# Attention's outputs packed by DMA and scaled by GpSimd, masks of bank-filling diagonals moved to VectorE, joined programs, and expert 0's places and lists first

## The chip, the cores and the metric

The kernel runs on one core of one Trainium2 chip, as one launch. The metric is the device time of that core in microseconds. Times of before come from three runs; the profile is of one further execution.

## The reference

Four residual blocks follow one another on x of shape [4, 1024, 256], each on a layer norm of x. The first is a mamba scan (512 inner channels, 16 states), the second a top-2 mixture of eight experts, the third causal attention with grouped heads, the fourth a mixture in which each expert takes its 256 best tokens per batch. Only the last two are touched:

```python
# attention: 16 query heads, 4 key heads, 16 channels each
q = rope((x @ Wqa @ Wqb).reshape(b, s, 16, 16)); k, v = ...   # k with rope
scores = where(causal, -inf, q @ k^T * 16 ** -0.5)
x = x + (softmax(scores) @ v).reshape(b, s, 256) @ Wout + bout
# experts: each of 8 takes its 256 highest tokens per batch
probs = softmax(layernorm(x) @ gate_w)
top_p, top_idx = top_k(probs transposed to [b, e, t], 256)
y = gelu(xn[top_idx] @ w1) @ w2 * top_p
x = x + zeros.at[top_idx].add(y)
```

## The kernel before

The kernel is written with one program per engine and semaphores between them; a stage is a block, and all engines meet at its end. Around some stages stands a `cleanup_on_exit`, which frees and resets what the stage held. The order of the work within a stage is written out by hand.

The stages are: mamba (to 1015 us of the span), the top-2 experts (to 1336), `norm_project` (norm, q, k, v and rope, written to DRAM in parts, to 1452), `attention` (1456 to 1953), `project_scores` (output projection, the next norm, gate scores, 1954 to 2013), and `choose_experts` (the search for each expert's threshold, places and lists, then the loop over eight experts, to the end).

**Attention** runs 16 units, one for each batch and key head (`w = 4 b + kv`), each with four query heads. A unit has 12 steps x: for the first half of the queries (h = 0) four key tiles, for the second half (h = 1) eight. At a step PE makes transposed scores for two pairs of heads (`scores_t`, L2293), ACT takes the exponential into `pt` (L2346), GpSimd cuts the future out of diagonal tiles (L2230), and PE weighs v with it into bank OB (`weigh_v`, L2309). Column 16 of v is one, so the sums come with the outputs, as the 17th of each head's 32 rows. At x = 4, and at x = 0 of the next unit, ACT copies the bank to `ot` [128, 1024] (`copy_out`, L2336), half at a time.

Between these, in three slots of each step, PE makes "pieces" for the next unit: untransposed scores of 512 columns or fewer in three banks (`maxima_scores`, L2249). A piece that touches a diagonal gets the mask added by a second matmul (L2252). DVE reduces each piece to a maximum (`take_max`, L2364) and frees its bank. `unit_events` lays the pieces and turns in order, and SHARES says how many events each step gets. Among the events are the two o_turns of a unit: PE transposes four 128x128 tiles of `ot` (`turn_out`, L2268), and DVE takes the reciprocal of the sums and multiplies (`divide_out`, L2394 and L2396) into `o_all` by rows of tokens. The maxima are cut into bf16 parts, sent to DRAM and back as extra rows of Q by SP (`send_maxima`, L2204 and L2206), and SP loads the heads of later units (`load_heads`).

**project_scores** turns each of the 32 tiles of `o_all` on PE (`turn_o`, L2479), ACT copies it (`copy_oT`, L2546), PE multiplies by w_out (`project`, L2487), and DVE adds to X and takes the statistics (L2593, L2597). PE may be two tiles ahead of the adds.

**choose_experts** searches the thresholds over 15 digits: DVE compares all tokens with three trial levels (L2948), in two halves of four tiles, PE counts by matmuls with ones (L2774), DVE picks the digit (L2951 to L2964). Then for all eight experts at once DVE finds members (L2971), PE ranks them (L2779, L2780), DVE makes places from these (L2979 to L3000) and, with GpSimd for the second half of the tokens, values (L3006, L3008; L3098, L3100). One-hots and lists for expert 0 follow (L3014, L2856), GpSimd gathers its rows (L3113), and PE begins the loop at L2799. That loop is bound by PE to the end.

Of the kernel before, what the change touches and what calls it, by code (L numbers as in the profile page):

```python
# [629 lines left out]
NE = 8  # L630
# [1089 lines left out]
def norm_project(nc, g, load_from, v_all, heads, q_dram, k_dram, weights, ahead):  # L1720
    with ExitStack() as ctx:
# [28 lines left out]
        t_psum, part_act, part_dve, out_sem = n.sem("t_psum"), n.sem("part_act"), n.sem("part_dve"), [n.sem(f"out_parts{i}") for i in range(2)]  # L1750
# [10 lines left out]
        def _(sp):  # L1761
# [34 lines left out]
            for s in range(2):  # L1796
                sp.wait_ge(out_sem[s], 8 * NB3 * NCH)

# [300 lines left out]
SHARES = (3, 3, 5, 2, 3, 5, 4, 4, 5, 3, 3, 2)  # L2099
SLOTS = 3  # L2100

# [5 lines left out]
def unit_events(w):  # L2107

    if w + 1 == NU:
        return [[[("m_turn", w, 1)], [], []], [[], [], [("o_turn", w - 1, 1)]]] + [[[], [], []] for _ in range(3)] + \  # L2110
            [[[], [], [("o_turn", w, 0)]]] + [[[], [], []] for _ in range(NSTEP - 6)]
    events = maxima_of(w + 1, 0) + maxima_of(w + 1, 1)
    events.insert(16, ("o_turn", w, 0))
    events.insert(18, ("m_turn", w + 1, 0))
    events.insert(1, ("m_turn", w, 1))
    events.insert(6, ("o_turn", w - 1, 1) if w else None)
    out, at = [], 0
    for share in SHARES:
        mine = events[at:at + share]
        out.append([[e for e in mine[share * i // SLOTS:share * (i + 1) // SLOTS] if e] for i in range(SLOTS)])  # L2120
        at += share
    assert at == len(events)
    return out

def schedule():

    units = [unit_events(w) for w in range(NU)]
    fill = maxima_of(0, 0) + [("m_turn", 0, 0)] + maxima_of(0, 1)
    ending = [("o_turn", NU - 1, 1)]  # L2130
    in_order = fill + [e for unit in units for step in unit for slot in step for e in slot] + ending
    return fill, units, ending, {e: k for k, e in enumerate(in_order)}

def attention_weights(n, g):
    mask_f = n.sb("mask_f", [P, P])
# [19 lines left out]
def attention(nc, g, v_all, heads, o_all, w_out, q_dram, k_dram, m_dram, weights):  # L2156
    with ExitStack() as ctx:
# [8 lines left out]
        ot = n.sb("ot", [P, SEQ])  # L2166
# [4 lines left out]
        inv = n.sb("inv", [P, KB, GH])  # L2171

# [10 lines left out]
        fill, in_unit, ending, order = schedule()  # L2183
# [15 lines left out]
        def _(sp):  # L2199
# [9 lines left out]
            send_maxima(0, 0)  # L2209
            sp.dma_start(w_out[:, :, :], g["wout"].rearrange("(k p) c -> p k c", p=P)).then_inc(w_loaded, 16)  # L2210
            for w in range(NU):
                send_maxima(w, 1)
                if w + NKV - 1 < NU:
# [3 lines left out]
                if w + 1 < NU:  # L2217
                    send_maxima(w + 1, 0)
            sp.wait_ge(w_loaded, 16)

        @block.gpsimd
        def _(pool):
            loads.wait(pool)
            for w in range(NU):
                for x in range(NSTEP):
                    if on_diagonal(x):
                        for pair in range(2):
# [3 lines left out]
                                               channel_multiplier=-1).then_inc(future_cut, 1)  # L2231
                for t in (2 * w, 2 * w + 1):
                    pool.tensor_tensor(X[:, t, :], X[:, t, :], bout[:, :], ALU.add).then_inc(x_biased, 1)

        @block.tensor
        def _(pe):
# [3 lines left out]
            def maxima_scores(w, h, i, k):  # L2240
# [5 lines left out]
                k0, diagonal = part * BANK, (tile + 1) * P - part * BANK <= BANK  # L2246
# [17 lines left out]
            def turn_out(w, h, k):  # L2264
                pe.wait_ge(ot_copied, 2 * w + h + 1)
                for i in range(4):
                    at = h * BANK + i * P
                    mm = pe.transpose(PS[:, k % NSB, i * P:(i + 1) * P], ot[:, at:at + P], ident[:, :])  # L2268
                mm.then_inc(piece_made, 1)

            def pieces(events):
                for e in events:
# [5 lines left out]
                    elif e[0] == "m_turn":  # L2278
                        turn_maxima(*e[1:], k)
                    else:  # L2280
                        turn_out(*e[1:], k)
# [16 lines left out]
            def weigh_v(w, x):  # L2298

                (b, kv), (h, kb) = divmod(w, NKV), STEPS[x]  # L2300
                if kb == 0 and (w or h):
                    pe.wait_ge(ot_copied, 2 * w + h)
# [24 lines left out]
            pieces(ending)  # L2327

        @block.scalar
        def _(act):  # L2330
            def copy_out(w, h):

                act.wait_ge(pv_done, NSTEP * w + (HK if h == 0 else NSTEP))
                if w:
                    act.wait_ge(o_step, 2 * w + h - 1)
                act.activation(ot[:, h * BANK:(h + 1) * BANK], PS[:, OB, :], ACT.Copy).then_inc(ot_copied, 1)  # L2336
# [18 lines left out]
        def _(dve):  # L2355
            dve.tensor_copy(ident_b[:, :], ident[:, :]).then_inc(consts, 1)
            loads.wait(dve)
            dve.tensor_copy(mask[:, :], mask_f[:, :]).then_inc(consts, 1)  # L2358
# [29 lines left out]
            def divide_out(w, h, k):  # L2388

                b, kv = divmod(w, NKV)  # L2390
                src = PS[:, k % NSB, :].rearrange("p (i j c) -> p i j c", i=4, j=GH)
                to = slice(h * 4, h * 4 + 4)
                tiles = slice(b * KB + h * 4, b * KB + h * 4 + 4)
                dve.reciprocal(inv[:, to, :], src[:, :, :, HD]).then_inc(o_step, 1)  # L2394
                dve.wait_ge(o_step, 2 * w + h + 1)
                dve.tensor_tensor(o_all[:, tiles, kv * GH * HD:(kv + 1) * GH * HD].rearrange("p i (j d) -> p i j d", j=GH),  # L2396
                                  src[:, :, :, 0:HD], inv[:, to, :, None].to_broadcast([P, 4, GH, HD]),
                                  ALU.mult).then_inc(piece_read, 1)

            def pieces(events):  # L2400
                for e in events:
# [6 lines left out]
                    elif e[0] == "m_turn":  # L2408
                        cut(*e[1:], k)
                    else:  # L2410
                        divide_out(*e[1:], k)
# [6 lines left out]
            pieces(ending)  # L2418

def project_scores(nc, g, o_all, w_out, xnT, xn_all, rows_to, gate, ahead):
    with ExitStack() as ctx:
# [3 lines left out]
        oT = n.sb("oT", [P, 2, KC, P])  # L2426
# [3 lines left out]
        oT_psum, oT_copied, o_psum, o_added = (n.sem(x) for x in ("oT_psum", "oT_copied", "o_psum", "o_added"))  # L2430
# [6 lines left out]
        TURN_BANKS, GB, OTB, OB = 3, 3, 4, 6  # L2437
# [36 lines left out]
        def _(pe):  # L2474
            def turn_o(t):
                if t >= 2:
                    pe.wait_ge(oT_copied, t - 1)
                for c in range(KC):
                    mm = pe.transpose(PS[:, OTB + t % 2, c * P:(c + 1) * P], o_all[:, t, c * P:(c + 1) * P], ident[:, :])  # L2479
                mm.then_inc(oT_psum, 1)  # L2480

            def project(t):
                pe.wait_ge(oT_copied, t + 1)
                if t >= 2:
                    pe.wait_ge(o_added, t - 1)
                for c in range(KC):
                    mm = pe.matmul(PS[:, OB + t % 2, 0:DM], oT[:, t % 2, c, :], w_out[:, c, :], start=c == 0, stop=c == KC - 1)  # L2487
# [36 lines left out]
            turn_o(0)  # L2524
            for t in range(NT):
                if t + 1 < NT:
                    turn_o(t + 1)
# [13 lines left out]
        def _(act):  # L2541
            def copy_oT(t):
                act.wait_ge(oT_psum, t + 1)
                if t >= 2:
                    act.wait_ge(o_psum, t - 1)
                act.activation(oT[:, t % 2, :, :].rearrange("p c x -> p (c x)"), PS[:, OTB + t % 2, 0:KC * P],  # L2546
# [768 lines left out]
```

## Time and profile before

| | us |
|---|---|
| median of 3 runs | 2563.05 |
| lowest, highest | 2562.51, 2564.99 |
| the profiled execution | 2565.26 |
| its span | 2563.5 |
| mean granted clock of PE over the span | 0.946 |

The profile is of a single execution. Instructions are named by engine, line and operation, with what they write and read. PE is the matmul engine, DVE VectorE, ACT ScalarE, POOL GpSimd, SP the engine that issues most DMAs. The start of an instruction is measured from the start of the span. PE's ends are modelled, so starts are surer than ends.

### The profile page before, as it was taken

The page shows a single profiled execution, that of the slowest core. Times are in us where ns is not written, and L with a number is a line of the kernel's source. Part 1 is how long each engine was busy: PE and PEld are TensorE (multiplying, and loading weights), DVE is VectorE, ACT ScalarE, POOL GpSimd, SP SyncE. Part 2 cuts the span into 40 slices and gives each one's busy share as a digit, 9 for nine tenths or more (in the row PEclk, how much of TensorE's full clock was granted, in tenths as well). Part 3 has the DMA queues.
Part 4 walks back from the last instruction along what each step waited for, and adds up shares of the span by engine and source line. Part 5 has one row for each costly group of instructions (what it writes and reads, how often), then busy time and mean ns, then how long its engine had stood idle before and what let it go on. Part 6 is the DMA issues. An engine that isn't in the chain of part 4 may idle for free. (4 is left out here: it accounts for less than half of the span.)

```text
span 2563.5 us, 35108 instructions
## 1 busy us (share of the span) xinstructions
PE 2265.3 (88%) x11484; PEld 1336.4 (52%) x11485; DVE 1779.8 (69%) x2586; ACT 1340.3 (52%) x2581; POOL 1346.8 (53%) x1026
## 2 busy tenths in 40 slices
PE   8995889989989987699977699999998559999998
PEld 3442444544544544699964344444445326666666
DVE  6998999999999997655557788888883741111100
ACT  4777887788788785322225456666665211111110
POOL 1545999899899894377756222222222123333432
PEclk9997999999999999799987799999999769999999
DMA  5357345125124113644446522222200503333322
GB/s 164 146 188 259 105 133 186 46 79 172 50 92 155 50 50 103 175 73 70 72 87 142 130 34 33 36 44 36 34 3 4 198 25 67 82 70 68 74 51 25
DMA packets 149681, 231.17 MB, mean 90 GB/s; under 512 B 26257, under 2 KB 98897, under 8 KB 149394
## 3 DMA queue, kind: packets, MB, share of 16 engines
q1 hardware_dynamic: 120258, 190.25, 24.7%
q0 software_dynamic: 29280, 39.11, 9.5%
q8 instruction: 79, 1.29, 0.2%
q14 instruction: 64, 0.52, 0.1%
HBM read 152.23 MB, written 81.66 MB: 91 GB/s over the span
## 5 line engine op out<-in xcount | busy, mean ns | idle before, releaser
L1263 POOL TENSOR_TENSOR scan_hC<-scan_h,scan_c_all 128x1024 f32<-128x1024 f32 x256 | 613.0, 2420 | 65.1 <-DVE scan_h L1118 63.8
L1118 DVE TENSOR_TENSOR_SCAN scan_h<-scan_dA,banks 128x1024 f32<-128x1024 f32 x224 | 504.6, 2276 | 21.6 <-ACT scan_dA L1040 12.9
L893 PE MATMUL banks<-scan_hC,all_ident 128*128 128x512 f32 x1024 | 487.5, 600 | 26.4 <-DVE scan_xc L1125 26.4
L2346 ACT ACTIVATE attn_pt<-banks 128x1024 f32<-128x1024 f32 (+3 forms) x384 | 292.3, 810 | 186.3 <-PE banks L2293 184.8
L1033 ACT ACTIVATE scan_scaled<-mamba_duT,mamba_bT 128x128 f32<-128x128 f32 x1024 | 312.0, 388 | 22.7 <-PE banks L870 22.3
L2230 POOL TENSOR_SCALAR_AFFINE_SELECT attn_pt<-attn_pt 128x256 f32<-128x256 f32 x256 | 104.2, 413 | 382.4 <-ACT attn_pt L2346 380.8
L2364 DVE TENSOR_REDUCE attn_m_lo<-banks 128x1 f32<-128x512 f32 (+3 forms) x432 | 266.8, 662 | 30.1 <-PE banks L2249 19.9
L893 PEld LDWEIGHTS banks<-scan_hC,all_ident 128*128 128x128 f32 x1024 | 185.3, 191 | 179.3 <-issue 129.2
L3068 DVE TENSOR_TENSOR ffn_y<-banks,ffn_gates 128x512 f32<-128x512 f32 x32 | 22.1, 692 | 334.2 <-PE banks L2828 327.5
L3124 POOL DMA_INDIRECT out<-ffn_y,ffn_ids x64 | 105.3, 1646 | 270.4 <-DVE ffn_y L3068 260.6
L2249 PE MATMUL banks<-attn_K,attn_Q 96*128 96x512 bf16 (+3 forms) x768 | 232.1, 340 | 11.1 <-DVE attn_mask L2358 10.0
L2812 PE MATMUL banks<-ffn_xgT,ffn_w 128*128 128x512 f32 x512 | 229.0, 599 | 0.8 <-issue 0.8
L2828 PE MATMUL banks<-ffn_w,ffn_hT 128*128 128x256 f32 x1024 | 228.6, 380 | 0.0
L2828 PEld LDWEIGHTS banks<-ffn_w,ffn_hT 128*128 128x128 f32 x1024 | 191.9, 190 | 28.5 <-issue 4.3
L2293 PE MATMUL banks<-attn_Q,attn_K 99*128 99x512 bf16 (+3 forms) x768 | 182.9, 327 | 1.2 <-ACT attn_pt L2346 1.1
L2886 ACT ACTIVATE ffn_hT<-banks 128x1024 f32<-128x1024 f32 x64 | 65.5, 1024 | 210.4 <-PE banks L2812 200.8
L870 PEld LDWEIGHTS banks<-all_ident,scan_scaled 128*128 128x128 f32 x1024 | 118.8, 144 | 104.2 <-DVE scan_h L1118 73.4
L2309 PE MATMUL banks<-attn_pt,attn_v_all 128*32 128x512 f32 (+3 forms) x1536 | 163.6, 498 | 0.7 <-POOL attn_pt L2230 0.6
L2249 PEld LDWEIGHTS banks<-attn_K,attn_Q 96*128 96x128 bf16 x768 | 74.2, 98 | 168.3 <-DVE attn_m_lo L2364 71.2
L870 PE MATMUL banks<-all_ident,scan_scaled 128*128 128x128 f32 x1024 | 141.5, 283 | 18.2 <-DVE scan_h L1118 16.7
L1040 ACT ACTIVATE scan_dA<-mamba_dt,mamba_a_neg 128x1024 f32<-128x1024 f32 x112 | 127.2, 1144 | 53.7 <-DVE scan_h L1118 46.0
L2812 PEld LDWEIGHTS banks<-ffn_xgT,ffn_w 128*128 128x128 f32 x512 | 96.1, 191 | 107.4 <-issue 106.7
(353 smaller groups left out, 3851.2 us busy)
## 6 DMA issues: line engine op xcount, KB each, us to landing
scan_c_all<-scratch_bc SPq DMA_DIRECT2D x64, 512.0 KB, 6.2
ffn_w<-in_e_w SPq DMA_DIRECT2D x16, 1024.0 KB, 5.4
attn_Q<-scratch_q SPq DMA_DIRECT2D x96, 128.0 KB, 4.1
scratch_x<-front_xc SPq DMA_DIRECT2D x8, 1024.0 KB, 5.8
scratch_z<-front_zs SPq DMA_DIRECT2D x8, 1024.0 KB, 7.5
scan_xc<-scratch_x SPq DMA_DIRECT2D x16, 512.0 KB, 3.7
scan_zs<-scratch_z SPq DMA_DIRECT2D x16, 512.0 KB, 4.7
scratch_dt<-front_lw SPq DMA_DIRECT2D x7, 1024.0 KB, 4.1
```

The costliest lines, as they stand in the source:

```text
L870: mm = pe.transpose(PS[:, (s % 2) * HALVES + half, i * P:(i + 1) * P], scaled[:, half * TPB // HALVES + i, :], ident[:, :])
L893: mm = pe.matmul(PS[:, YB + i, :], ident[:, :], hC[:, u % NHC, i * BANK:(i + 1) * BANK], start=s == 0, stop=s == NST - 1, skip_group_check ...
L1033: op = act.activation(scaled[:, t, :], duT[:, t, :], ACT.Copy, scale=bT[:, t, i:i + 1])
L1118: dve.tensor_tensor_scan(h[:, u % NH, :], decay, drive, 0.0, ALU.mult, ALU.add).then_inc(scanned, 1)
L1263: pool.tensor_tensor(hC[:, u % NHC, :], h[:, u % NH, :], c_all[:, s, :], ALU.mult).then_inc(hC_done, 1)
L2249: mm = pe.matmul(PS[:, k % NSB, at:at + width], Q[0:KR, kv, j0 + z, tile * P:(tile + 1) * P], K[0:KR, kv, k0:k0 + width], start=True, stop ...
L2293: mm = pe.matmul(PS[:, ST + 2 * pair + z, 0:BANK - lo], K[:, kv, kb * P:(kb + 1) * P], Q[:, kv, 2 * pair + z, h * BANK + lo:(h + 1) * BANK ...
L2309: mm = pe.matmul(PS[j * VW:(j + 1) * VW, OB, lo:BANK], v_all[:, b * KB + kb, kv, :], pt[:, (NSTEP * w + x) % 4, j, 0:BANK - lo], start=kb ...
L2346: act.activation(pt[:, at % 4, 2 * pair:2 * pair + 2, 0:width], PS[:, ST + 2 * pair:ST + 2 * pair + 2, 0:width], ACT.Exp, scale=HD ** -0.5 ...
L2364: dve.tensor_reduce(dst, PS[:, k % NSB, 0:nj * width].rearrange("p (j x) -> p j x", j=nj), AX, ALU.max).then_inc(piece_read, 1)
L2812: mm = pe.matmul(PS[:, HB + (hp % 2) * 2 + i, :], w1[:, s, k, (2 * hp + i) * P:(2 * hp + i + 1) * P], xgT[:, pr, k, :], start=k == 0, stop ...
L2828: mm = pe.matmul(PS[:, YB + z, hf * DM:(hf + 1) * DM], hT[:, pr, c, j * P:(j + 1) * P], w2[:, s, c, :], start=c == 0, stop=c == HC - 1, sk ...
```

## The change

1. **Outputs of attention.** `turn_out` and `divide_out` are gone from attention, `turn_o` and `copy_oT` from project_scores. A class `HeadOutputs` takes their place. SP sends `ot` of a unit to DRAM (`send`, 512 KB) and takes it back by eight DMAs (`take`): the 16 rows of each head into `dense`, which has channels on partitions, and the row of sums, repeated over 16 partitions, into `sums`. DVE inverts `sums` in place, 64 partitions × 1024 elements (`invert`), for unit w − 2 after step x = 4 of unit w; the last two after tiles 8 and 12 of project_scores. GpSimd multiplies (`scale`), at the same place in its own order, and the last two at the head of project_scores. ACT's `copy_out` waits for the last unit's store. `project` reads `dense` as it is and waits, every eight tiles, until four units are scaled.
2. **Masks.** For pieces whose diagonal ends with the bank (tiles 3 and 7, eight pieces a unit) PE adds no mask; DVE does both in one tensor_tensor_reduce with a mask of 512 columns, of which the first 384 are zero.
3. **Wait moved.** SP's wait for norm_project's stores stands now in attention, ahead of the load of w_out.
4. **Choice.** The trial is compared in 6 + 2 tiles. `places(q)` runs for expert 0 alone, then for the other seven; between them stand expert 0's lists. All values are made on DVE.
5. **Programs.** top2, attention and lists stand in one cleanup instead of three.

```diff
@@ def unit_events(w):
     events = maxima_of(w + 1, 0) + maxima_of(w + 1, 1)
-    events.insert(16, ("o_turn", w, 0))
-    events.insert(18, ("m_turn", w + 1, 0))
+    events.insert(17, ("m_turn", w + 1, 0))
     events.insert(1, ("m_turn", w, 1))
-    events.insert(6, ("o_turn", w - 1, 1) if w else None)
-SHARES = (3, 3, 5, 2, 3, 5, 4, 4, 5, 3, 3, 2)
+SHARES = (3, 3, 4, 2, 3, 4, 4, 4, 5, 3, 3, 2)
+class HeadOutputs:
+    def send(self, sp, w):
+        sp.wait_ge(self.copied, 2 * w + 2)
+        sp.dma_start(self.dram[w, :, :], self.ot[:, :]).then_inc(self.put, 16)
+    def take(self, sp, w):
+        b, kv = divmod(w, NKV)
+        sp.wait_ge(self.put, 16 * (w + 1))
+        if w >= 2:
+            sp.wait_ge(self.scaled, w - 1)
+        for j in range(GH):
+            first = kv % 2 * GH * HD + j * HD
+            to = slice(first, first + HD)
+            sp.dma_start(self.dense[to, kv // 2, b * SEQ:(b + 1) * SEQ], self.dram[w, j * VW:j * VW + HD, :]
+                         ).then_inc(self.taken[w % 2], 16)
+            sp.dma_start(self.sums[to, :], self.dram[w, j * VW + HD:j * VW + HD + 1, :].to_broadcast([HD, SEQ])
+                         ).then_inc(self.taken[w % 2], 16)
+    def invert(self, dve, w):
+        rows = slice(w % 2 * GH * HD, (w % 2 + 1) * GH * HD)
+        dve.wait_ge(self.taken[w % 2], 16 * 2 * GH * (w // 2 + 1))
+        dve.reciprocal(self.sums[rows, :], self.sums[rows, :]).then_inc(self.inverted, 1)
+    def scale(self, pool, w):
...
+        pool.wait_ge(self.inverted, w + 1)
+        pool.tensor_tensor(own, own, self.sums[rows, :], ALU.mult).then_inc(self.scaled, 1)
+        pool.wait_ge(self.scaled, w + 1)
@@ attention, SP
             send_maxima(0, 0)
+            for out in out_sem:
+                sp.wait_ge(out, 8 * 3 * NCH)
             sp.dma_start(w_out[:, :, :], g["wout"].rearrange("(k p) c -> p k c", p=P)).then_inc(w_loaded, 16)
             for w in range(NU):
                 send_maxima(w, 1)
+                if w:
+                    outs.send(sp, w - 1)
...
                 if w + 1 < NU:
                     send_maxima(w + 1, 0)
+                if w:
+                    outs.take(sp, w - 1)
@@ attention, GpSimd
+                    if x == HK and w >= 2:
+                        pool.wait_ge(future_cut, cuts_through(w, x))
+                        outs.scale(pool, w - 2)
@@ attention, PE
-                k0, diagonal = part * BANK, (tile + 1) * P - part * BANK <= BANK
+                k0, diagonal = part * BANK, (tile + 1) * P - part * BANK < BANK
@@ attention, ACT
-                    act.wait_ge(o_step, 2 * w + h - 1)
+                    act.wait_ge(outs.put, 16 * w)
@@ attention, DVE
+                if (tile + 1) * P - part * BANK == BANK:
+                    src = PS[:, k % NSB, :]
+                    dve.tensor_tensor_reduce(src, src, mask_f[:, :], 1.0, LOWEST, ALU.add, ALU.max, dst).then_inc(piece_read, 1)
+                    return
...
                     for slot in in_unit[w][x]:
                         pieces(slot)
-            pieces(ending)
+                    if x == HK and w >= 2:
+                        outs.invert(dve, w - 2)
@@ project_scores
             def project(t):
-                pe.wait_ge(oT_copied, t + 1)
+                if t % TPB == 0:
+                    pe.wait_ge(outs.scaled, NKV * (t // TPB + 1))
...
                 add_o(t)
                 if t:
                     count(t - 1)
+                if t in (8, 12):
+                    outs.invert(dve, NU - 2 + (t == 12))
@@ choose_experts
-        HI = TPB // 2
+        HI = 6
...
-            dve.wait_ge(lane_made, 1)
+            places(0)
             first_lists(0)
             first_lists(1)
+            places(1)
@@ the kernel
-        with nc.cleanup_on_exit():
-            o_all, w_out = attention_layer(nc, g, load_from=x)
-        with nc.cleanup_on_exit():
-            lists_layer(nc, g, o_all, w_out, out)
+            outs, w_out = attention_layer(nc, g, load_from=x)
+            lists_layer(nc, g, outs, w_out, out)
```

## Rows read from the trace of the kernel before

**Rows 1.** The page, part 1: busy time of each engine.

```profile
PE 2265.3 (88%) x11484; PEld 1336.4 (52%) x11485; DVE 1779.8 (69%) x2586; ACT 1340.3 (52%) x2581; POOL 1346.8 (53%) x1026
```

**Rows 2.** Busy time by window: stretch, length, PE, PEld, DVE, ACT, POOL, PEclk, DMA, GB/s.

```profile
1670.57:1700.27 29.70, 29.55 (x236) 12.76 (x234) 26.54 (x52) 19.14 (x28) 7.89 (x18) 1.00 0.23 35
```

**Rows 3.** Single instructions at program edges: start, length, engine, line, [idle before <- released by].

```profile
1451.03 0.73 SPq L1785 DMA_DIRECT2D scratch_k<-proj_parts  x1
...
1456.45 1.28 ACT L2346 ACT_TABLE_LOAD   x1 [7.34 <-PEq L1721]
...
1952.21 0.42 DVE L2396 TENSOR_TENSOR attn_o_all<-banks,attn_inv 128x256 f32<-128x256 f32 x1
...
1953.76 0.41 SPq L52 DMA_DIRECT2D moe2r_gate_w<-in_gate  x1
...
1955.72 1.11 PE L2479 MATMUL banks<-all_ident,attn_o_all 128*128 128x128 f32 x4 [3.85 <-DMA moe2r_gate_w<-in_gate]
...
2011.88 0.65 PE L2520 MATMUL banks<-all_ident,oln_lt 128*128 128x128 f32 x4 [0.71 <-ACT oln_lt L2566]
...
2012.82 0.38 SPq L2750 DMA_DIRECT2D out<-all_X  x1
...
2084.58 1.11 PE L2799 MATMUL banks<-all_ident,ffn_xg 128*128 128x128 f32 x4 [5.96 <-DMA ffn_xg<-scratch_xn_rows,ffn_ids]
```

**Rows 4.** Single instructions of PE in an attention unit, at x = 4.

```profile
1671.59 0.22 PE L2252 MATMUL banks<-attn_mask,attn_ident_b 128*128 128x128 bf16 x1
1671.65 0.60 PE L2268 MATMUL banks<-all_ident,attn_ot 128*128 128x128 f32 x4
...
1672.19 1.06 PE L2309 MATMUL banks<-attn_pt,attn_v_all 128*32 128x512 f32 x8
```

**Rows 5.** Groups by form, DVE's reciprocals: count | busy us, mean ns | idle before.

```profile
L2932 DVE RECIPROCAL choose_total<-choose_total 128x32 f32<-128x32 f32 x1 | 0.4, 353 | 0.0
L2620 DVE RECIPROCAL oln_rstd<-oln_rstd 128x4 f32<-128x4 f32 x2 | 0.3, 169 | 0.3 <-ACT oln_rstd L2552 0.3
L2620 DVE RECIPROCAL oln_rstd<-oln_rstd 128x16 f32<-128x16 f32 x1 | 0.2, 235 | 0.0
L2620 DVE RECIPROCAL oln_rstd<-oln_rstd 128x8 f32<-128x8 f32 x1 | 0.2, 185 | 0.0
```

**Rows 6.** Groups by form: long instructions of DVE and GpSimd.

```profile
L1263 POOL TENSOR_TENSOR scan_hC<-scan_h,scan_c_all 128x1024 f32<-128x1024 f32 x256 | 613.0, 2420 | 65.1 <-DVE scan_h L1118 63.8
L1118 DVE TENSOR_TENSOR_SCAN scan_h<-scan_dA,banks 128x1024 f32<-128x1024 f32 x224 | 504.6, 2276 | 21.6 <-ACT scan_dA L1040 12.9 <-PE banks L870 0.6
L2364 DVE TENSOR_REDUCE attn_m_lo<-banks 128x1 f32<-128x512 f32 x320 | 203.4, 682 | 22.8 <-PE banks L2249 19.9 <-PE banks L2252 2.9
L500 DVE SCALAR_TENSOR_TENSOR banks<-front_xpad,mamba_taps,banks 128x512 f32<-128x512 f32 x64 | 48.4, 756 | 2.3
```

**Rows 7.** Busy time by window, as in rows 2: stretches after an idle PE.

```profile
1955.75:1961.40 5.65, 5.60 (x17) 4.27 (x18) 0.69 (x2) 1.15 (x3) 0.00 (x0) 0.50 0.08 14
...
1378.96:1384.60 5.64, 5.64 (x18) 4.14 (x19) 2.31 (x5) 2.79 (x9) 5.64 (x7) 0.50 1.11 257
```

**Rows 8.** The page, part 6: DMA issues, KB each, us to landing.

```profile
scan_c_all<-scratch_bc SPq DMA_DIRECT2D x64, 512.0 KB, 6.2
```

**Rows 9.** Single instructions of PE in project_scores, one tile.

```profile
1973.11 0.38 PE L2479 MATMUL banks<-all_ident,attn_o_all 128*128 128x128 f32 x2
1973.33 0.38 PE L2487 MATMUL banks<-attn_w_out,oln_oT 128*128 128x256 f32 x1
```

**Rows 10.** Single instructions of DVE and PE in the choice.

```profile
2031.58 1.03 DVE L2948 TENSOR_TENSOR choose_above<-choose_probs,choose_trial 128x384 bf16<-128x384 f32 x2
2032.19 0.97 PE L2774 MATMUL banks<-choose_above,choose_ones_b 128*128 128x96 bf16 x8 [1.75 <-DVE choose_above L2948]
...
2058.71 0.88 DVE L2971 TENSOR_TENSOR choose_member<-choose_probs,choose_level 128x256 f32<-128x256 f32 x2
...
2068.32 0.42 DVE L3006 TENSOR_TENSOR moe_vals<-choose_inside,moe2r_place 128x256 bf16<-128x256 f32 x1
```

More of the change, by code:

```diff
@@ L2119, in unit_events @@
         mine = events[at:at + share]
-        out.append([[e for e in mine[share * i // SLOTS:share * (i + 1) // SLOTS] if e] for i in range(SLOTS)])
+        out.append([mine[share * i // SLOTS:share * (i + 1) // SLOTS] for i in range(SLOTS)])
         at += share
@@ L2129, in schedule, with __init__ @@
     fill = maxima_of(0, 0) + [("m_turn", 0, 0)] + maxima_of(0, 1)
-    ending = [("o_turn", NU - 1, 1)]
-    in_order = fill + [e for unit in units for step in unit for slot in step for e in slot] + ending
-    return fill, units, ending, {e: k for k, e in enumerate(in_order)}
+    in_order = fill + [e for unit in units for step in unit for slot in step for e in slot]
+    return fill, units, {e: k for k, e in enumerate(in_order)}
+class HeadOutputs:
+    def __init__(self, nc, n):
+        right = lambda name, shape: nc.alloc_sbuf_tensor(f"attn_{name}", shape, F32, side="right")
+        self.dense, self.ot, self.sums = right("o_dense", [P, KC, TOK]), right("ot", [P, SEQ]), right("sums", [P, SEQ])
+        self.dram = scratch(nc, "o", [NU, P, SEQ])
+        self.copied, self.put, self.inverted, self.scaled = (n.sem(x) for x in ("ot_copied", "o_put", "inverted", "scaled"))
+        self.taken = [n.sem(f"o_taken{i}") for i in range(2)]
+    def send(self, sp, w):
[18 more added lines that the diff above has]
+    def scale(self, pool, w):
+        b, kv = divmod(w, NKV)
+        rows = slice(kv % 2 * GH * HD, (kv % 2 + 1) * GH * HD)
+        own = self.dense[rows, kv // 2, b * SEQ:(b + 1) * SEQ]
+        pool.wait_ge(self.inverted, w + 1)
+        pool.tensor_tensor(own, own, self.sums[rows, :], ALU.mult).then_inc(self.scaled, 1)
+        pool.wait_ge(self.scaled, w + 1)
@@ L2182, in attention @@
         NSB, ST, OB = 3, 3, 7
-        fill, in_unit, ending, order = schedule()
+        fill, in_unit, order = schedule()
         def on_diagonal(x):
@@ L2417, in _, with project_scores @@
                         pieces(slot)
-            pieces(ending)
-def project_scores(nc, g, o_all, w_out, xnT, xn_all, rows_to, gate, ahead):
+                    if x == HK and w >= 2:
+                        outs.invert(dve, w - 2)
+def project_scores(nc, g, outs, w_out, xnT, xn_all, rows_to, gate, ahead):
     with ExitStack() as ctx:
@@ L2486, in project @@
                 for c in range(KC):
-                    mm = pe.matmul(PS[:, OB + t % 2, 0:DM], oT[:, t % 2, c, :], w_out[:, c, :], start=c == 0, stop=c == KC - 1)
+                    mm = pe.matmul(PS[:, OB + t % 2, 0:DM], outs.dense[:, c, t * P:(t + 1) * P], w_out[:, c, :], start=c == 0, stop=c == KC - 1)
                 mm.then_inc(o_psum, 1)
@@ L2645, in _ @@
         def _(pool):
+            outs.scale(pool, NU - 2)
+            outs.scale(pool, NU - 1)
             for k, (first, last) in enumerate(GROUPS[:3]):
@@ L2945, in _ @@
                 dve.wait_ge(leveled, 6 * k + 2)
-                for half in range(2):
-                    at = slice(half * HI, (half + 1) * HI)
+                for at in PIECES_OF_TRIAL:
+                    cut = [P, TRIALS, BATCH, at.stop - at.start, NE]
                     dve.tensor_tensor(above[:, :, :, at, :], by_batch[:, None, :, at, :].to_broadcast(cut),
@@ L3240, in attention_layer @@
         heads = (Q, K, q_in)
+        out_sem = [na.sem(f"out_parts{i}") for i in range(2)]
         for_attention = attention_weights(na, g)
@@ L3265, in lists_layer @@
                 gate = gate_weights(nx, g["gate2"])
-                project_scores(nc, g, o_all, w_out, xnT, xn_all, xn_rows, gate, ahead=(gate[-1], consts[-1]))
+                project_scores(nc, g, outs, w_out, xnT, xn_all, xn_rows, gate, ahead=(gate[-1], consts[-1]))
             choose_experts(nc, g, lane, vals, xn_rows, out_rows, consts)
```

227 lines of the change are left out of this document (95 added, 132 removed).

## The prediction

> **What bounds the kernel now.** I read four views. The page's first part: PE is busy for 88% of the span [rows 1]. The busy times by window, of one attention unit: 16 units follow one another at 29.7 us, PE is busy for 29.55 of it at full clock, DVE for 26.54, POOL for 7.89 [rows 2]. So PE bounds attention, but DVE has only 3.2 us of slack per unit, less than one long instruction could need. Groups by form then give DVE prices, and the list of single instructions gives the edges between programs, where every engine stands: norm_project's last DMA is issued at 1451.76 and attention begins at 1456.45; attention's last multiply ends at 1952.63, the first DMA of project_scores is issued at 1953.76, PE starts only at 1955.72; its last matmul ends at 2012.53 and the next block begins at 2012.82 [rows 3]. From 2084.58 [rows 3] the experts run as before; that stage moves only as a whole. The profiled execution took 2565.26 us (span 2563.5), 2.2 over the median of 2563.05. I work out differences on it and take them off the median.
>
> **PE's work in a unit.** Removed: eight transposes of ot (L2268). Four take 0.60 us from first start to last end, one some 0.27, so they start (0.60 − 0.27)/3 = 0.11 apart [rows 4]: 8 × 0.11 = 0.87. Removed too: the mask matmul of the eight pieces whose diagonal ends with the bank; the next instruction starts 0.06 after a mask's start [rows 4]: 8 × 0.06 = 0.46. Together 1.33, so a unit of PE work falls from 29.69 to 28.36. That is worth 13 × 1.33 = 17.3 in units 2 to 14, and 2.2 in units 0 and 1 together, since unit 0 has one turn fewer.
>
> **DVE's work in a unit.** Removed: two pairs, each a 128x16 reciprocal (0.24 [rows 5]) and a multiply (0.42 [rows 3]), 1.3 in all. Eight reduces of 0.68 become a tensor_tensor_reduce that also reads a mask from SBUF. No row shows this form. The nearest with two tensor operands over 512 elements of a bank is L500 at 0.756 [rows 6]; from above a scan costs 2.276 for 1024, or 1.14 for 512 [rows 6]. A gain is excluded, since it reads more than the reduce does. I take 0.69 to 0.76, up to 0.6 per unit, because the operation has no dependence of one element on the last. At 1.14 it is +3.7 per unit. With the taken value DVE needs about 25.6 without the new reciprocal.
>
> **The new reciprocal.** Each unit from w = 2 runs one DVE reciprocal over 64 partitions × 1024 elements, after step x = 4, and two more stand in project_scores. The old ones had 16 elements. The groups by form give the price per element: 169 ns for 4, 185 for 8, 235 for 16, 353 for 32 [rows 5], so 4.0, 6.3 and 7.4 ns for each further element, the rise flattening. At 7.4 the 1024 take 0.35 + 992 × 0.0074 = 7.7 us; rises of 2.3 and 1.1, halving, lead to a limit near 8.5 ns and 8.8 us. I take R = 8.5. The bound from below is that the short forms are all fixed cost and a long one streams like a reduce, 0.68 for 512 [rows 6], R = 1.4. I go by the slope, as it grows with length and doesn't fall.
>
 The trace's slope of 7.4 ns at 32 elements is on its way to that 8.3; no row of before is long enough to show it.
>
> **What waits for it.** DVE also empties PE's three piece banks. While it inverts, PE can do the pieces of three banks, the scores of the next step and one weigh_v; 512 columns at 2.4 GHz are 0.21, so a bank is 0.27 with its mask, the two score pairs are 0.86, and the weigh_v group lasts 1.06 [rows 4]: 0.81 + 0.86 + 1.06 = 2.7, and DVE starts 1.0 after PE's last piece of x = 4 and needs 0.7 for the first bank afterwards. PE then stands for 1.0 + R + 0.04 + 0.68 − 2.7 = R − 0.98 = 7.5 us. DVE's slack after the stall doesn't give it back, since PE is the bound of the rest of the unit. So 13 units (w = 2 to 14) cost 13 × 7.5 = 97.8. In unit 15 no pieces are left, and nobody waits.
>
> **The clock after a stall.** PE's granted clock was 0.50 from 1955.75 to 1961.4 [rows 7] after PE had been idle for 3.85 us [rows 3]; it was 0.50 also from 1378.96 to 1384.6, after an idle stretch as well [rows 7]. In a unit, which has no such stretch, it is 1.00 [rows 2]. The two levels are 1.2 and 2.4 GHz. 5.7 us at half clock lose 2.85 where PE is the bound; a part overlaps waits, and I take 2.6 for each of 13 + 2 stalls: 39. The ends are 0 (the clock holds) and 3.4.
>
> **Outputs by DMA.** ot (512 KB a unit) goes to DRAM and back by nine DMAs. A 512 KB load lands after 6.2 us [rows 8]. ACT's copy at x = 4, 9 us after the last, waits for the store; the store's issue follows the x = 0 copy and stands behind send_maxima on SP, 3.4 into the unit, and lands 4 to 6 later, so 7.8 to 10.3 against 9.3. The overshoot, 0 to 1 us, lies under the invert's stall from unit 2 on; I take 0. POOL multiplies 64x1024: L1263 takes 2.42 for 128x1024 [rows 6], and POOL idles for 21.8 of 29.7 [rows 2]; nothing waits, so 0. SP's wait for norm_project's stores moves ahead of w_out's load, a load that nobody needs before 1953: 0, and its 4.7 (1451.76 to 1456.45) falls to a plain block change of 0.3 (2012.53 to 2012.82): −4.3 [rows 3].
>
> The Trainium skill ("GPSIMD Engine Reference", section "1. Specifications") says that GpSimd shares its SBUF interfaces with VectorE and contends with DVE instructions of two SBUF inputs; here DVE's reduces read PSUM, so it would add nothing beside the scale, and no row of a unit shows such contention.
>
> **Joined programs.** Two cleanups go: 1952.63 to 1953.76 is 1.13 against 0.3 for a plain change [rows 3], 0.85 each: −1.7. The ending transposes and divide after the last weigh_v: −1.5.
>
> **project_scores.** The 32 turned tiles are gone: 0.22 each between a transpose's start and the next matmul's, 1973.11 to 1973.33 [rows 9], 6.9, and 0.6 of bubbles: −7.5. New: the inverts at t = 8 and 12 hold up DVE's adds, which PE needs two tiles later: 2 × (R − 1.7) = +13.6.
>
> **Choosing.** Search: compares in 6 + 2 tiles instead of 4 + 4. Two compares take 1.03, the count starts 0.61 after the first compare's start and takes 0.97 with a pause inside [rows 10]. With six tiles it starts 0.24 later and loses the 0.17 of pause: +0.08 for each of 15 digits, +1.3; ends −1 and +2. Places and lists of expert 0 first: members to lane took 2058.71 to 2068.32, 9.6 us of 128x256 instructions [rows 10]; an eighth as wide each costs mostly its fixed time, about 4.4, −5.2; its vals fall from 3.2 to 0.9, and without POOL beside them one-hots gain 0.7: −8.2 in all. The other seven experts' places then run on DVE while PE waits for the gather that ends at 2084.58 [rows 3]; they end about 2084 before the shift. That is the thin cover: if they end later, PE's wait for places_read costs the difference, up to 4.
>
> **Sum.** Gains: −17.3 − 2.2 + 0.4 (slower reduces in the DVE-bound fill) − 4.3 − 1.7 − 1.5 − 7.5 + 1.3 − 8.2 = −41.0. Costs: 97.8 + 13.6 + 39 = +150.4. Net +109.4: 2563 + 109 = **2672** (on the profiled run 2675). Without other cases its range is 2655 to 2705, from R 7.7 (−12), R 8.8 (+5), clock, and choosing.
>
> **Rivals.**
> 1. The stalls come, but the clock stays at 1.00, since half a unit of dense work lies between them. Against it: the clock fell after 3.85 us of idling [rows 3, 7], half my stall. For it: only stretches of another shape show it. −41 + 97.8 + 13.6 = +70.4: 2633, 2615 to 2650.
> 2. The long reciprocal is cheap. At R = 1.4 the stall is 0.3, nearly no clock is lost: 2563 − 41 + 4 = 2526. Between both stands the point of no change: 15R − 16.1 = 41, R = 3.8 us, where the change turns from a gain to a loss. The four forms speak against it. This is the other side: faster.
> 3. Everything dear: R = 8.8, 3.4 of clock lost each time, the reduce with mask at 1.14, which makes DVE catch up late: +109 + 5 + 12 + 14 = 2704 and above.
> 4. The change doesn't do what it says: the stall disappears because invert's place lets PE run further ahead, or R is near 3.8: within 5 us of before.
>
> **Chances.** Forecast 0.62, rival 1 0.20, rival 2 0.08, rival 3 0.08, rival 4 0.02. The range leaves out rival 2, 4 and the tail of 3: 2612 to 2704. Faster by over 0.2% (5 us, what a measurement can tell here) 0.08, within 0.02, slower 0.90.
>
> **What would show it.** Right: a DVE RECIPROCAL 64x1024 of 7.7 to 8.8 us, some 14 in attention; behind each an idle time of PE of 7 to 8 us put down to a DVE piece; granted clock 0.5 for 5 to 6 us after it; units 2 to 14 at 38.5 us; no L2268, the edges of 0.85 and 4.7 gone; experts start 8 us sooner after project_scores. Wrong: R off the slope moves the result by 15 us for each us, and is the step on which sign and size hang; a unit of 36 says that the clock held; a unit above 40 with DVE busy throughout says that the reduce with mask is dear.

## The result, and the profile after

The changed kernel takes 2641.0 us (median of 4 runs, 2639.85 to 2643.14); before took 2563.67 in the runs beside it. The ratio is 1.0302, 95% interval 1.0285 to 1.0320: 77 us slower. The forecast was 2672, range 2612 to 2704. Its own range without other cases, 2655 to 2705, doesn't hold 2641. The profiled execution took 2641.87 us, its span 2640.2.

The page, part 1, of the changed kernel answers [rows 1]: PE's share fell and DVE's rose by 90 us of work.

```profile
PE 2281.3 (86%) x11166; PEld 1322.2 (50%) x11167; DVE 1870.2 (71%) x2686; ACT 1329.2 (50%) x2549; POOL 1378.4 (52%) x1040
```

Busy time by window of the changed kernel, columns as in [rows 2]: one unit, then the stall in it, then the stretch behind.

```profile
1789.83:1826.97 37.14, 31.44 (x220) 12.01 (x219) 32.38 (x57) 19.13 (x28) 10.12 (x19) 0.86 0.30 57
1801.20:1806.50 5.30, 0.00 (x0) 0.00 (x0) 5.27 (x3) 0.00 (x0) 0.56 (x1) 0.66 0.35 41
1806.70:1812.40 5.70, 5.70 (x21) 1.65 (x20) 3.70 (x9) 2.05 (x2) 1.58 (x1) 0.50 0.02 5
```

This unit takes 37.1 us, where one of before took 29.7; the mean of units 2 to 14 is 36.4. For 5.3 of these PE does nothing while DVE is busy throughout, and for the next 5.7 PE is busy at a granted clock of 0.50. Single instructions of DVE, and then of PE, show what DVE was busy with:

```profile
1799.24 6.55 DVE L2159 RECIPROCAL attn_sums<-attn_sums 64x1024 f32<-64x1024 f32 x1
1805.83 0.69 DVE L2398 TENSOR_REDUCE attn_m_lo<-banks 128x1 f32<-128x512 f32 x1
```

```profile
1800.75 0.39 PE L2289 MATMUL banks<-attn_K,attn_Q 96*128 96x512 bf16 x1
1806.57 0.38 PE L2301 MATMUL banks<-all_ident,attn_m_lo 128*16 128x128 f32 x1 [5.44 <-DVE attn_m_lo L2398]
```

PE fills its third piece bank at 1800.75. It is idle for 5.44 us, until the reduce behind the reciprocal empties the oldest bank. From 1534 to 1971, the waits name the same pair twelve times (the first number is the sum, the last the longest):

```profile
PE banks L2301 <- DVE attn_m_lo L2398: 62.8, 12, 5.4
```

Groups by form of DVE, the new work beside the old reduce of [rows 6]:

```profile
L2398 DVE TENSOR_REDUCE attn_m_lo<-banks 128x1 f32<-128x512 f32 x256 | 165.6, 681 | 37.9 <-PE banks L2289 37.0
L2159 DVE RECIPROCAL attn_sums<-attn_sums 64x1024 f32<-64x1024 f32 x16 | 104.7, 6541 | 0.2
L2396 DVE CUSTOM_DVE_ANT_0 banks<-banks,attn_mask_f 128x512 f32<-128x512 f32 x128 | 85.8, 714 | 8.0 <-PE banks L2289 7.6
L2396 DVE DVE_READ_ACCUMULATOR2_ANT attn_m_hi<- 128x1 f32 x64 | 9.1, 142 | 0.0
```

The edges, as single instructions; they answer [rows 3]:

```profile
1448.76 0.66 SPq L1785 DMA_DIRECT2D scratch_k<-proj_parts  x1
...
1450.07 1.28 ACT L2376 ACT_TABLE_LOAD   x1 [3.25 <-PEq L1721]
...
2032.75 3.78 PE L2503 MATMUL banks<-attn_w_out,attn_o_dense 128*128 128x256 f32 x8 [3.14 <-DMA moe2r_gate_w<-in_gate]
...
2095.25 0.66 PE L2536 MATMUL banks<-all_ident,oln_lt 128*128 128x128 f32 x4 [0.71 <-ACT oln_lt L2572]
...
2159.72 1.12 PE L2818 MATMUL banks<-all_ident,ffn_xg 128*128 128x128 f32 x4 [1.87 <-DMA ffn_xg<-scratch_xn_rows,ffn_ids]
```

By stage, from these traces (us):

| stretch of PE | before | changed | difference |
|---|---|---|---|
| start to the first piece of attention | 1456.95 | 1450.57 | −6.4, of which about 4 is the moved wait |
| from there to the last weigh_v | 493.5 | 579.0 | +85.5 |
| to the first work in project_scores | 5.3 | 3.1 | −2.1 |
| project_scores | 56.8 | 63.2 | +6.3 |
| to the experts' first matmul | 72.0 | 63.8 | −8.2 |
| the experts, to the end of the span | 478.9 | 480.5 | +1.6 |

The sum is +76.7, as is the difference of the spans. In project_scores PE stands twice, for one reciprocal each:

```profile
2051.12 5.84 PE L2503 MATMUL banks<-attn_w_out,attn_o_dense 128*128 128x256 f32 x16 [5.84 <-DVE all_X L2598]
2062.78 2.50 PE L2503 MATMUL banks<-attn_w_out,attn_o_dense 128*128 128x256 f32 x5 [5.83 <-DVE all_X L2598]
```

### The profile page after: what moved, and what is told of

Read it like the earlier page. It is cut to its first block and busy times, and to the rows that moved or that the text cites. A ratio compares the mean times of both kernels' runs of the same rounds, so it can differ in the third digit from the quotient of the medians.

```text
span 2640.2 us, 34625 instructions
## 1 busy us (share of the span) xinstructions
PE 2281.3 (86%) x11166; PEld 1322.2 (50%) x11167; DVE 1870.2 (71%) x2686; ACT 1329.2 (50%) x2549; POOL 1378.4 (52%) x1040
## 5 line engine op out<-in xcount | busy, mean ns | idle before, releaser
L2398 DVE TENSOR_REDUCE attn_m_lo<-banks 128x1 f32<-128x512 f32 (+3 forms) x368 | 228.0, 657 | 44.3 <-PE banks L2289 37.0
L2289 PE MATMUL banks<-attn_K,attn_Q 96*128 96x512 bf16 (+3 forms) x768 | 243.6, 355 | 6.9 <-DVE attn_mask L2388 5.9
L2324 PE MATMUL banks<-attn_Q,attn_K 99*128 99x512 bf16 (+3 forms) x768 | 197.3, 347 | 1.4 <-ACT attn_pt L2376 1.2
L2340 PE MATMUL banks<-attn_pt,attn_v_all 128*32 128x512 f32 (+3 forms) x1536 | 173.1, 524 | 0.8 <-POOL attn_pt L2267 0.6
```

The costliest lines, as they stand in the source:

```text
L2289: mm = pe.matmul(PS[:, k % NSB, at:at + width], Q[0:KR, kv, j0 + z, tile * P:(tile + 1) * P], K[0:KR, kv, k0:k0 + width], start=True, stop ...
L2324: mm = pe.matmul(PS[:, ST + 2 * pair + z, 0:BANK - lo], K[:, kv, kb * P:(kb + 1) * P], Q[:, kv, 2 * pair + z, h * BANK + lo:(h + 1) * BANK ...
L2340: mm = pe.matmul(PS[j * VW:(j + 1) * VW, OB, lo:BANK], v_all[:, b * KB + kb, kv, :], pt[:, (NSTEP * w + x) % 4, j, 0:BANK - lo], start=kb ...
```

## The experiments

Where the expectations name 2641, 28.4 and 36.4 us, these are the measured time of the changed kernel, the unit by PE's work alone, and its measured unit.

### The reciprocal replaced by a copy

```diff
-        dve.reciprocal(self.sums[rows, :], self.sums[rows, :]).then_inc(self.inverted, 1)
+        dve.tensor_copy(self.sums[rows, :], self.sums[rows, :]).then_inc(self.inverted, 1)
```

> The changed kernel with each long reciprocal replaced by a copy of the same 64x1024 elements in place, so the attention outputs are multiplied by the sums and not divided: the division is left out. My theory: the stall behind the reciprocal and the slow clock after it are the whole loss. Then units 2 to 14 fall from 36.4 to about 28.4 us, 13 x 8.0 = 104, and project_scores loses its two stalls, 14 more: 2641 - 118 = 2523 us, granted clock 1.00 in the units, 1.5% below the kernel before. Rival (something else is hidden under the stall: the store and loads of ot, GpSimd's scale, the reduce with mask): units stay at 29.7 or above, 2540 us or more.

Measured: 2523.2 us, ratio 0.9844 (0.9827 to 0.9860); this kernel leaves the division out. One unit, by window:

```profile
1678.20:1706.65 28.45, 28.20 (x220) 11.44 (x219) 26.15 (x57) 19.02 (x28) 10.14 (x19) 1.00 0.37 75
```

The unit is 28.45 us, at clock 1.00. So 118 us (2641.0 less 2523.2) hang on the reciprocal alone; the store and loads of ot, GpSimd's scale and the fused reduces cost nothing beside PE. All the rest of the change together is worth −40.7 us against the 2563.9 of before beside it.

### The reciprocal over a part of the elements

Three kernels, with 384, 512 and 768 of the 1024 elements; in each the rest of the sums stays uninverted.

```diff
-        dve.reciprocal(self.sums[rows, :], self.sums[rows, :]).then_inc(self.inverted, 1)
+        dve.reciprocal(self.sums[rows, 0:SEQ // 2], self.sums[rows, 0:SEQ // 2]).then_inc(self.inverted, 1)
```

> The changed kernel with the reciprocal over 512 of the 1024 elements of each row; the other half of the sums isn't inverted. By 6.54 us for 1024 and 0.35 for 32 elements one takes 6.2 ns per element, so 3.35 us, and my formula R - 0.98 gives a stall of 2.4 us per unit. If the clock falls after a stall this short as it did after the long one (2.6 us lost each), units are 28.4 + 2.4 + 2.6 = 33.4 and the time about 2523 + 13 x 5.0 + 9 = 2597 us. If the clock holds, units are 30.8 and the time about 2523 + 13 x 2.4 + 3 = 2557 us: then the loss isn't proportional to the reciprocal and half of it gives no loss against before.

> The changed kernel with the reciprocal over 384 of 1024 elements of each row, the rest of the sums isn't inverted. By 3.34 us for 512 and 6.54 for 1024, 6.25 ns per element, R = 2.54 and the stall R - 0.98 = 1.56 us. If PE's granted clock holds after stalls this short, each of the units 2 to 14 takes 28.45 + 1.56 = 30.0 us and the time is 2523 + 13 x 1.56 + 2 = 2545 us. If the clock still falls in some units, as after the stalls of 1.9 to 2.2 us with 512 elements, some units show 31.5 and the time is 2550 to 2562 us. The point of no change against before then lies between this size and 512 elements.

> The changed kernel with the reciprocal over 768 of 1024 elements of each row, the rest isn't inverted. R = 4.94, stall 3.96 us. With a low clock of 5 to 7 us in every unit, 2.4 us each, units take 34.8 and the time is 2523 + 13 x 6.35 + 9 = 2615 us. If the loss of clock goes with the length of the stall, it is 1.7 each, as seen with 512 elements, and the time 2606 us or below.

Measured: 384 elements 2548.6 us, ratio 0.9945 (0.9928 to 0.9961); 512 elements 2573.65, 1.0042 (1.0025 to 1.0059); 768 elements 2608.7, 1.0178 (1.0161 to 1.0195). The reciprocals, by form, one kernel each:

```profile
L2159 DVE RECIPROCAL attn_sums<-attn_sums 64x384 f32<-64x384 f32 x16 | 40.7, 2541 | 0.2
```

```profile
L2159 DVE RECIPROCAL attn_sums<-attn_sums 64x512 f32<-64x512 f32 x16 | 53.5, 3343 | 0.3
```

```profile
L2159 DVE RECIPROCAL attn_sums<-attn_sums 64x768 f32<-64x768 f32 x16 | 79.1, 4942 | 0.3
```

From 384 to 1024 elements this is (6541 − 2541) / 640 = 6.25 ns for each element, with 0.14 us at zero. Now a unit of each, by window: 384, then 512 (two units), then 768.

```profile
1655.92:1685.89 29.97, 28.59 (x220) 11.28 (x219) 27.83 (x57) 19.01 (x27) 10.12 (x19) 1.00 0.38 71
```

```profile
1566.06:1597.06 31.00, 28.51 (x220) 11.28 (x219) 28.80 (x57) 19.03 (x28) 10.15 (x19) 1.00 0.31 69
1660.35:1692.52 32.17, 29.98 (x220) 11.73 (x219) 28.82 (x57) 19.12 (x27) 10.15 (x19) 0.95 0.35 66
```

```profile
1568.70:1602.85 34.15, 30.06 (x220) 11.43 (x219) 30.49 (x57) 19.14 (x28) 10.13 (x19) 0.95 0.30 62
```

With R the length of the reciprocal, the first is 28.45 + 1.5, where R − 0.98 gives 1.56; the second 28.45 + 2.55, where it gives 2.36. Neither lost any clock. PE idles some 0.3 us longer in units with odd w than in those with even w, and with it go the two lengths. The third is one of even w at a mean clock of 0.95. One of even w at clock 1.00 takes 30.77 in the same trace, so here the clock's price is seen by itself: 1.4 us.

With 384 elements one of 13 units showed a slow clock, with 512 eight, with 768 and 1024 all. So the 2573.65 for 512 lies between the 2557 expected if the clock holds and the 2597 if it falls. The expected 2615 for 768 was too high, since ten of its units lost 1.4 to 1.7 us and not 2.4. With 1024 a unit takes 36.43 us on average and lost 7.98 − 5.56 = 2.4. Between 384 and 512 the change turns from a gain to a loss: on the straight line between them the time of before is met at R = 3.0 us, where I had 3.8 with the clock left out.

### The same reciprocal in eight parts

```diff
+    def invert_part(self, dve, w, i):
+        rows = slice(w % 2 * GH * HD, (w % 2 + 1) * GH * HD)
+        at = slice(i * SEQ // 8, (i + 1) * SEQ // 8)
+        dve.wait_ge(self.taken[w % 2], 16 * 2 * GH * (w // 2 + 1))
+        dve.reciprocal(self.sums[rows, at], self.sums[rows, at]).then_inc(self.inverted, 1)
...
-                    if x == HK and w >= 2:
-                        outs.invert(dve, w - 2)
+                        if x < HK and w >= 2 and z != 1:
+                            outs.invert_part(dve, w - 2, 2 * x + (z == 2))
```

> The changed kernel with each unit's reciprocal in attention cut into eight of 64x128, two in each of the steps 0 to 3 ahead of where the long one stood (the last two in project_scores are still whole). DVE does at least as much work: 8 x 0.95 = 7.6 us for 6.54. Theory of the clock (one long idle stretch of PE lets the granted clock fall): PE now waits in pieces of about 1 us, the clock stays at 1.00, the unit is 28.4 plus 4 to 5 us of waits, 33.2, and the time 2523 + 13 x 4.8 + 14 = 2599 us. Rival (the loss is DVE's work alone, wherever it stands): units at 36 or above, 2641 or more.

Measured: 2621.0 us, ratio 1.0226 (1.0209 to 1.0243), 20 less than in one piece, 22 more than I expected. Two units that follow one another:

```profile
1673.73:1707.01 33.28, 29.23 (x220) 11.29 (x219) 31.50 (x64) 19.45 (x28) 10.17 (x19) 1.00 0.33 64
1707.01:1744.49 37.48, 32.38 (x220) 12.02 (x219) 33.77 (x64) 19.45 (x27) 10.15 (x19) 0.91 0.26 56
```

Seven of 13 units, those with even w, are 33.28 us, about the number I had put down (33.2), at clock 1.00. The six between them are 35.9 or 37.5, at 0.91 in the one shown. So the waits were right, and that splitting keeps the clock was wrong: short waits also let it fall, in every other unit. The two kinds differ in their waits. With even w PE waits 0.56, 0.65, 0.23, 0.65, 1.21 and 0.50 us, and the clock stays. With odd w it waits 1.09 and 0.95 within 2.7 us, and the low clock begins at the end of the second or 1 us later. Why these waits are longer with odd w isn't shown. The rival, DVE's work alone at 36 us or above, falls too: 33.28 with all of that work stands in the same run.

### The sums inverted before they are repeated

The 4096 sums of a unit are different numbers, which the change repeats over 16 partitions and only then inverts. Here they are laid out as 128x32, inverted, stored, and repeated by the loads.

```diff
+            sp.dma_start(self.raw[j * 32:(j + 1) * 32, w % 2, :],
+                         self.dram[w, j * VW + HD, :].rearrange("(p x) -> p x", p=32)).then_inc(self.taken[w % 2], 16)
...
-        dve.reciprocal(self.sums[rows, :], self.sums[rows, :]).then_inc(self.inverted, 1)
+        dve.reciprocal(self.raw[:, w % 2, :], self.raw[:, w % 2, :]).then_inc(self.inverted, 1)
+
+    def spread(self, sp, w):
+        sp.wait_ge(self.inverted, w + 1)
+        sp.dma_start(self.inv_dram[w, :, :].rearrange("j (p x) -> (j p) x", p=32), self.raw[:, w % 2, :]).then_inc(self.stored, 16)
+        sp.wait_ge(self.stored, 16 * (w + 1))
+        if w >= 2:
+            sp.wait_ge(self.scaled, w - 1)
+        for j in range(GH):
+            first = w % 2 * GH * HD + j * HD
+            sp.dma_start(self.sums[first:first + HD, :], self.inv_dram[w, j:j + 1, :].to_broadcast([HD, SEQ])
+                         ).then_inc(self.there[w % 2], 16)
```

> The changed kernel, with the sums of a unit laid out by DMA as 128x32 and inverted before they are repeated over 16 partitions: one reciprocal of 0.35 us per unit, then a 16 KB store and four loads that repeat each row, one unit later, and GpSimd's scale one unit later. My theory: as in the run with a copy, units at 28.4 us, 2520 to 2527 us in all, faster than both kernels. Rival: SP now waits for the inverse and for its store between send_maxima and the next take, so the heads or maxima of later units come late, or the last unit's way through four DMAs holds up project_scores: 2540 or more, with PE waiting on attn_Q or in project_scores at tile 24.

Measured: 2524.6 us, ratio 0.9846 (0.9830 to 0.9862). The reciprocal by form, and one unit:

```profile
L2159 DVE RECIPROCAL attn_raw<-attn_raw 128x32 f32<-128x32 f32 x16 | 5.5, 344 | 0.0
```

```profile
1678.20:1706.65 28.45, 28.19 (x219) 11.43 (x218) 25.65 (x57) 19.02 (x26) 10.16 (x20) 1.00 0.35 76
```

It is as fast as the copy, within the runs' spread, with the whole computation. SP's extra waits held up next to nothing: 12 of 13 units take 28.45 or 28.46 us, unit 2 takes 28.7. The rival falls.

### That version with the trial cut 4 + 4 again

```diff
-        HI = 6
+        HI = TPB // 2
```

> The version with the unique sums inverted, and the trial of the search cut 4 + 4 again. By the search's stretch in the traces (39.3 against 39.8 us) this is 0.5 us faster than with 6 + 2; by my prediction's term 1.3 us. Both lie below what three rounds tell apart, so the trace's stretch of the counts decides: 39.3 us if the cut is the cause, 39.8 if not. Time 2522 to 2526 us, as before it.

Measured: 2522.0 us, ratio 0.9834 (0.9819 to 0.9849), the lowest median of all. Its difference from 2524.6 is within the runs' spread, so the total decides nothing. The traces do. From the first count to the last it is 39.4 us here and 39.3 before, and 39.8 in every trace with 6 + 2; and PE waits 5.76 us for the first count here and before, and 5.97 with 6 + 2. So the 6 + 2 cut costs 0.7 us.

### Masks alone, choice alone, joined programs alone

Each is one part of the change on the kernel before. Masks:

```diff
-                k0, diagonal = part * BANK, (tile + 1) * P - part * BANK <= BANK
+                k0, diagonal = part * BANK, (tile + 1) * P - part * BANK < BANK
...
+                if (tile + 1) * P - part * BANK == BANK:
+                    src = PS[:, k % NSB, :]
+                    dve.tensor_tensor_reduce(src, src, mask_f[:, :], 1.0, LOWEST, ALU.add, ALU.max, dst).then_inc(piece_read, 1)
+                    return
```

> The kernel before with only the masks of the bank-filling diagonals moved to DVE. In the changed kernel the fused instruction shows 0.715 us and a read of its accumulator of 0.14 behind it, 0.86 for the reduce's 0.68: DVE 26.5 + 8 x 0.18 = 28.0 us per unit, PE 29.69 - 0.46 = 29.2. Theory: PE stays the bound, units at 29.2, 15 x 0.46 = 7 us less, 2557 us. Rival: at 28 of 29.2 us DVE is late at places where pieces stand close, and gives back half or all of it, 2560 to 2567, or is slower than before.

Measured: 2558.7 us against 2564.6, ratio 0.9979 (0.9970 to 0.9988): −5.9. A unit is 29.33 us, so the masks give 0.36 and not 0.46. DVE's work is 26.81 us for 26.54 before [rows 2], and not the 28.0 I expected:

```profile
1669.65:1698.98 29.33, 29.07 (x227) 12.25 (x226) 26.81 (x60) 19.13 (x26) 7.82 (x18) 1.00 0.24 36
```

Choice, the whole of part 4 of the change, of which a few lines:

```diff
-        HI = TPB // 2
+        HI = 6
...
+            places(0)
             first_lists(0)
             first_lists(1)
+            places(1)
```

> The kernel before with only the choice of experts changed (trial in 6 + 2 tiles, expert 0's places first, all values on DVE). Theory: search +0.5 us (39.3 to 39.8 in the trace of the changed kernel), from the last count to the experts' first matmul 26.9 to 18.0: -8.4 in all, 2555 us. Rival: the seven experts' places on DVE run into expert 0's work and the loop gives some of it back: 2559 or more.

Measured: 2555.6 us, ratio 0.9967 (0.9954 to 0.9979): −9.0. The experts' first matmul waits 1.87 us for the gather, where it waited 5.96 [rows 3]:

```profile
2073.49 1.11 PE L2810 MATMUL banks<-all_ident,ffn_xg 128*128 128x128 f32 x4 [1.87 <-DMA ffn_xg<-scratch_xn_rows,ffn_ids]
```

Joined programs with the moved wait:

```diff
+            for out in out_sem:
+                sp.wait_ge(out, 8 * 3 * NCH)
...
-        with nc.cleanup_on_exit():
             o_all, w_out = attention_layer(nc, g, load_from=x)
-        with nc.cleanup_on_exit():
             lists_layer(nc, g, o_all, w_out, out)
```

> The kernel before with only the wait for norm_project's stores moved into attention and the three programs joined. Theory: 4.1 us less between norm_project's last matmul and attention's first, and 0.5 to 0.85 at each of two joints, -5.5: 2558 us. Rival: the stores' landing is waited for anyway by the loads of unit 0's heads, so only the joints gain: 2562.

Measured: 2560.0 us, ratio 0.9982 (0.9973 to 0.9991): −4.6. PE's first piece of attention and its first work in project_scores:

```profile
1451.93 0.27 PE L2248 MATMUL banks<-attn_K,attn_Q 96*128 96x128 bf16 x1 [5.95 <-DVE attn_mask L2357]
...
1951.00 1.11 PE L2478 MATMUL banks<-all_ident,attn_o_all 128*128 128x128 f32 x4 [3.67 <-DMA moe2r_gate_w<-in_gate]
```

PE idles for 5.95 us where it idled for 10.03, so the wait is worth 4.1. At the joint before project_scores PE's idle time falls by 0.2 only, from 3.85 to 3.67. The load that PE waits for is issued 0.28 us after the last multiply's end, where it was issued 1.13 us after it [rows 3]. So the joint gave its 0.85 us, but in this one trace PE starts 2.6 us after the load's issue, for 2.0 before. In the changed kernel it is 1.9.

## Why the prediction was right, and where it was off

**The sign and the mechanism were right.** A DVE reciprocal of 1024 elements stops PE, which bounds the unit; the copy in its place gives 2523, the same kernel otherwise. The sizes that were to show it weren't met: 6.54 us for 7.7 to 8.8, an idle PE of 4.9 to 5.4 for 7 to 8, units of 36.4 for 38.5.

**The stall's formula held.** R − 0.98 was to be the idle time. With the measured R of 6.54 it is 5.56; the trace shows one idle stretch of 4.9 to 5.4 in each unit, and units at full clock grew by 1.5 to 1.7 with 384 elements and 2.3 to 2.55 with 512, for 1.56 and 2.36. In project_scores I had R − 1.7 = 4.8 for each of the two, and PE idled for 5.84 twice, 1.0 more than the formula gives.

**R itself was the term mis-sized: 8.5 for 6.54 us.** The step that was off is the slope: I took the differences of neighbouring forms in [rows 5] (4.0, 6.3, 7.4 ns), read their rise as a trend and let it go on to 8.5. The experiments show one straight line, 0.14 us + 6.25 ns per element. It gives 0.34 for 32, 0.24 for 16, 0.19 for 8 and 0.17 for 4, that is each of the four rows within 0.013 us. The rise was a scatter of some 10 ns in short instructions. A line through the ends of those rows, (353 − 169) / 28 = 6.6 ns, would have led to 6.9 us and a sum of +85. The surplus in R, 1.96 us, comes in 15 times: 29.4 of the 32 us by which the size missed (+109.4 for +77.3). The Trainium skill's repeat count of 8 ("VectorE: DVE Perf Modes", section "First, the fixed hardware budget") had seemed to support the limit. Measured are 6.25 ns. As an estimate from that page's 0.96 GHz this is six cycles, not eight, and the measurement decides.

**The clock.** I had 2.6 us lost per stall. The changed kernel's units lose 36.43 − 28.45 − 5.56 = 2.4 on average by the formula; by PE's busy time, 30.9 us for 28.2 with the copy, it is 2.7. The rival that the clock holds falls for 1024 elements and holds in 12 of 13 units for 384. My reason against it was a single idle stretch of 3.85 us, and the turning point lay below it, at 1.4 to 2.2 us of idling. My sign for this rival, a unit of 36 us, was a bad one: the units are 36.4 and their clock did fall. With R at 6.54 stall and slow clock together make 36.4, and only the granted clock tells the two cases apart.

**The rest, −41.0, measured −40.7 with the copy in place.** The total is closer than its parts, which is partly luck. Each part's time has an interval of about 2 to 3 us to either side, which holds the forecast; the traces tell where the terms erred, and they erred both ways:

| part | forecast | measured alone |
|---|---|---|
| masks | −6.5 (0.46 a unit) | −5.9 (0.36 a unit) |
| wait moved, programs joined | −6.0 | −4.6 |
| choice | −6.9 | −9.0 |
| outputs by DMA, without stalls | −21.6 | −21.2 (not measured alone: −40.7 less the three) |

The fused reduce shows 0.71 us and an accumulator read of 0.14, but these don't add up: where DVE has several in a row, they start 0.65 us apart, and plain reduces 0.60. That is 0.05 more for each, for an expected 0.01 to 0.08, and a unit of the masks alone has 0.3 us more of DVE's work. It had the room, since DVE has 28.45 for 26.15 of work.

The cleanup's 0.85 at project_scores was 0.2 in the one trace of the joined programs, for the load that took longer. The search was +0.7 and not +1.3. From the last count to the experts the choice gave 8.9, for 8.2. The places of the other seven held up the experts by 0.8 us at most in the kernel with the choice alone (479.8 for 478.9), where I had allowed for 4. In project_scores the version with a copy takes 47.0 us for 56.8, −9.8 and not −7.5.

**The range** held the time because rival 1 widened it downwards, and that was luck: 2641 lies in rival 1's 2615 to 2650, but its mechanism, a clock that holds, isn't what happened. The likeliest case's own range didn't hold it: its lower end, R = 7.7, was itself made with the last neighbour's slope. The bound from below was R = 1.4, and the gap between 1.4 and 7.7 was left to no case but rival 4's R near 3.8.

**Slips in the sums,** all small: at R = 1.4 the formula gives 0.42 and not 0.3, which makes rival 2 some 2 us slower; 32 times 0.22 is 7.0 and not 6.9; rival 3 adds up to 2703.

Open: the experts took 1.6 us longer in the changed kernel's trace. They took 480.6 with the joined programs alone, 479.8 with the choice alone and 478.7 with the masks alone, for 478.9 before. So joining goes with most of it; why isn't shown.

## What to carry to other kernels

Before an operation is widened by repeating its inputs, count the distinct values: 4096 sums inverted as 128x32 cost 0.34 us where the repeated 64x1024 cost 6.54, on an engine that another one waits for within 3 us. Take an unknown length's price from a line through all known lengths, and test it against each, rather than from the last two. A stall on the bounding engine can cost more than its length: here 1.4 us and more of slow clock came on top in most units from 2 us of idling on.

## What the runs showed of the hardware

DVE's reciprocal takes 0.14 us + 6.25 ns for each element of a partition (0.344 us for 32, 6.541 for 1024), where a copy of the same 64x1024 takes 0.68. PE's granted clock fell to 0.50 (1.2 for 2.4 GHz) in each unit with one idle stretch of 4.9 to 5.4 us, in each with 3.4 to 3.8, in eight of 13 with 1.9 to 2.2, and in one of 13 with 1.1 to 1.4; and, in every other unit of the split reciprocal, with waits of 1.09 and 0.95 us that followed one another closely. DVE's fused add and maximum of 128x512 with its accumulator read takes 0.65 us from start to start, a plain reduce of as many elements 0.60. GpSimd's 64x1024 product took 2.34 us, for 2.42 with twice the partitions [rows 6].
